# Gated delta stage re-staged: output product one stage later, first transposes last, two decay buffers; layer norms in two halves

## The reference

```python
mixed = silu(causal_conv4(hidden_states @ w_qkv)); z = hidden_states @ w_z
q = l2norm(q) * DK ** -0.5;  k = l2norm(k)          # over 128, per token and head
def step(Sm, inp):
    q_, k_, v_, g_, b_ = inp
    Sm = Sm * jnp.exp(g_)[..., None, None]
    kv = jnp.einsum('bhk,bhkv->bhv', k_, Sm)
    delta = (v_ - kv) * b_[..., None]
    Sm = Sm + jnp.einsum('bhk,bhv->bhkv', k_, delta)
    o = jnp.einsum('bhk,bhkv->bhv', q_, Sm)
    return (Sm, o)
og = o * silu(z);  on = og * rsqrt(mean(og * og) + EPS) * norm_w
return on.reshape(B, S, VAL_DIM) @ w_out
```

## Time and profile before

| | |
|---|---|
| median of three runs | 5708.66 us |
| profiled execution, its own time | 5727.5 us, span 5725.7 us |
| mean granted TensorE clock | 0.916 of full speed |
| PE busy | 4930.2 us, 86% of the span |
| DVE, ACT, POOL busy | 58%, 45%, 23% |
| the 64 stages | from about 200 to 3050 us |
| the eight layer norms | some 18 us each |

### The profile page before, as it was taken

The page is one execution under the profiler, slowest core; times in us unless marked ns, Lnnn a source line. Parts: engine busy times, 40 slices in busy tenths (PEclk is TensorE's granted clock), DMA queues, the critical chain, the costliest instruction groups (busy, mean ns, idle before and its releaser), DMA issues. The chain is left out here.

```text
span 5725.7 us, 125133 instructions
## 1 busy us (share of the span) xinstructions
PE 4930.2 (86%) x50094; PEld 3447.6 (60%) x50094; DVE 3347.2 (58%) x6298; ACT 2561.0 (45%) x6894; POOL 1319.4 (23%) x1478
## 2 busy tenths in 40 slices
...
GB/s 83 16 20 21 19 20 19 20 20 19 20 19 20 20 21 18 19 20 20 22 17 49 1 1 69 1 1 0 0 21 14 15 1 13 23 1 1 1 23 15
DMA packets 50618, 103.88 MB, mean 18 GB/s; under 512 B 12832, under 2 KB 20192, under 8 KB 48768
## 3 DMA queue, kind: packets, MB, share of 16 engines
...
## 5 line engine op out<-in xcount | busy, mean ns | idle before, releaser
L1034 DVE SCALAR_TENSOR_TENSOR dh_kq<-bank,dh_conv_kq,dh_kq 128x511 f32<-128x511 f32 (+2 forms) x408 | 305.3, 748 | 180.7 <-ACT dh_kq L850 169.6
L1034 DVE SCALAR_TENSOR_TENSOR dh_v<-bank,dh_conv_v,dh_v 128x511 f32<-128x511 f32 (+2 forms) x384 | 285.8, 748 | 169.9 <-ACT dh_v L850 159.9
L596 PE MATMUL bank<-hT,dh_w_kq 128*128 128x512 f32 x544 | 277.6, 635 | 49.3 <-DVE dh_kq L1034 42.3
L1247 POOL TENSOR_TENSOR dh_pto<-dh_qkm,dh_et 128x512 f32<-128x512 f32 x128 | 160.4, 1274 | 647.5 <-PE bank L572 647.5
L596 PE MATMUL bank<-hT,dh_w_vz 128*128 128x512 f32 x512 | 264.1, 641 | 51.0 <-DVE dh_v L1034 51.0
L1101 DVE TENSOR_TENSOR dh_turned<-dh_turned,bank 128x256 f32<-128x256 f32 x384 | 153.8, 414 | 246.8 <-ACT dh_turned L895 245.1
L1776 PE MATMUL bank<-moe_h_split,moe_w 128*128 128x512 bf16 x1200 | 277.2, 381 | 14.3 <-PEq L89 14.3
L766 PE MATMUL bank<-dh_wo_gated,dh_ww 128*128 128x256 f32 x1040 | 272.6, 421 | 0.8 <-ACT dh_ww L941 0.8
L259 POOL TENSOR_TENSOR ln_rstd<-ln_var_eps,nhalf 128x16 f32<-128x16 f32 x8 | 23.2, 2903 | 1018.3 <-DVE ln_var_eps L249 1018.3
L608 PE MATMUL bank<-dh_w_vz,hT 128*128 128x256 f32 x1024 | 245.5, 383 | 0.0
L766 PEld LDWEIGHTS bank<-dh_wo_gated,dh_ww 128*128 128x128 f32 x1040 | 214.2, 211 | 38.3 <-issue 1.1
...
## 6 DMA issues: line engine op xcount, KB each, us to landing
...
moe_w<-in_L_w13T SPq DMA_DIRECT2D x1, 3200.0 KB, 16.1
...
```

What stands on the lines that cost most here:

```text
L596: last = pe.matmul(pj_bank(n), w[:, kk, :], k.hT[:, kk, n % NB, :], start=(kk == 0), stop=(kk == KD - 1))
L1034: dve.scalar_tensor_tensor(y, pj_bank(n)[:, 0:S - i], taps(n)[:, TAPS - 1 - i:TAPS - i], y, ALU.mult, ALU.add).then_inc(s["v_cs" if i < TA ...
L1247: pool.tensor_tensor(pto[j][:, :, :], qkm[:, :, :], et[j][:, :, :], ALU.mult).then_inc(h["p_pt"], 1)
```

## The change

It computes the same. In the delta stages:
- `w_out(t - 1)` and `collect(t - 1)` stand in stage t, behind its first `next_power` and `next_turned`; they stood at the end of stage t - 1. An epilogue does the last.
- `flip(t)` and `turned_start` stand at the end of stage t, ahead of `y_turn`; they stood at the start of stage t + 1. `flip` writes the other bank (`turn_bank`).
- `decay` works in place on one of two buffers `et`, and stands in mid-stage; it stood ahead of `kk_mask` and `start_power`, read `inj` and wrote one buffer.
- `norms` is gone. `squares` does four ACTIVATEs with an accumulated sum, into `ss`, in place of one; no DVE work is left in it.
- The corner's matmuls alternate between two 64x64 tiles of the array, one for each head; both heads' matmuls ran on one tile, one head behind the other. For head 1 a third copy in `diagonal` is new.
- The filler stands in other places: `project(0)` and `project(1)` ahead of `v_turn`, `project_z(4)` and `(5)` in kind 3 (they were in kind 2), `turn_kq` 4 to 7 at the end of kind 3 (they were spread over it).

In `layernorm`, statistics, variance and the power on POOL are done for eight tiles, then for the other eight.

```diff
     def flip(pe, t):
         for j in HEADS:
-            after(pe, hs[j]["v_u"], t)
-            after(pe, hs[j]["a_u12"], t)
+            pe.wait_ge(hs[j]["v_u"], order(t) + 1)
+            after(pe, hs[j]["a_xs"], t + 1)
...
     def corner(pe, t):
...
-            for b in range(NB):
-                last = pe.matmul(pow_bank(j)[LO, b, :], off[j][HI, b, :], ttb[j][HI, b, HI], start=True, stop=True)
+        for b in range(NB):
+            for j in HEADS:
+                moved = c_even[j][LO, b, :] if j else ttb[j][HI, b, HI]
+                last = pe.matmul(pow_bank(j)[halves[j], b, :], off[j][halves[1 - j], b, :], moved, start=True, stop=True)
         last.then_inc(s["t_u12"], 1)
...
     def v_turn(pe, t, j):
-        after(pe, s["v_acc"], t)
+        pe.wait_ge(s["v_acc"], t + 1)
...
     def squares(act, q, n):
         if n < NC - 1:
-            act.activation(kt[:, par, n, :, :], b4(PJ_B), ACT.Copy)
-        if q >= 0:
-            act.wait_ge(s["t_wo"], NC * q + (2 if n < NC else 3))
-        after(act, s["v_ss"], N - 1)
-        act.activation(ww[n % 2][:, :, :], b4(PJ_B), ACT.Square).then_inc(s["a_sq"], 1)
+            act.activation(kt[:, par, n, :, :], b4(PJ_B), ACT.Copy).then_inc(s["a_kt"], 1)
+            act.wait_ge(s["a_kt"], (NC - 1) * max(q, 0) + n + 1)
+        for b in range(NB):
+            last = act.activation(b4(PJ_B)[:, b, :], b4(PJ_B)[:, b, :], ACT.Square,
+                                  accum_out=ss[:, par, n // NC, n % NC, b:b + 1])
+        last.then_inc(s["a_sq"], 1)
...
     def diagonal(act, t, j):
         for half in halves:
             last = act.activation(ttb[j][half, :, half], pow_bank(j)[half, :, :], ACT.Copy)
+        if j:
+            last = act.activation(c_even[j][LO, :, :], pow_bank(j)[HI, :, :], ACT.Copy)
...
     def decay(dve, t, j):
-        after(dve, h["p_nt"], t + 1)
-        after(dve, h["p_pt"], t + 1)
-        dve.tensor_tensor_scan(et[j][:, :, :].rearrange("p b n -> p (b n)"), ar[j][:, :],
-                               inj[j][:, :, :].rearrange("p b n -> p (b n)"), 0.0, ALU.mult, ALU.add)\
-            .then_inc(h["v_et"], 1)
+        dve.tensor_tensor_scan(e, ar[j][:, :], e, 0.0, ALU.mult, ALU.add).then_inc(h["v_et"], 1)
...
     def vector_stage(dve, t):
-        if a == 0: convolve(dve, q, 0)
-        if a == 1: scaled_out(dve, q)
-        if a == 2: convolve(dve, q, 12)
         for j in HEADS: grow(dve, t, 0, j)
+        if a == 1: scaled_out(dve, q)
+        collect(dve, t - 1)
+        if a == 0:
+            convolve(dve, q, 0)
+            convolve(dve, q, 1)
+        if a == 2: convolve(dve, q, 12)
+        for j in HEADS: grow(dve, t, 1, j)
+        if a:
+            for j in HEADS: decay(dve, t, j)
         if old:
             for j in HEADS: rhs(dve, t, j)
```

More of the change, by code:

```diff
@@ L495, in delta_pipeline @@
     per = lambda name: [sb(f"{name}{j}", [P, NB, P]) for j in HEADS]
-    inj, et, vs, ttb = per("inj"), per("et"), per("vs"), per("ttb")
+    et = [[sb(f"et{i}{j}", [P, NB, P]) for j in HEADS] for i in range(2)]
+    vs, ttb = per("vs"), per("ttb")
     pto, x0, zz, ww, yy, St = per("pto"), per("x0"), per("zz"), per("ww"), per("yy"), per("S")
@@ L680, in inverse @@
         for b in range(NB):
-            for j in HEADS:
-                at = halves[j]
-                last = pe.matmul(turn_bank(j)[LO, b, 0, :], c_odd[j][at, b, :], turn[j][at, TS[5], b, :], start=True, stop=True)
+            for at, j in zip(halves, HEADS):
+                last = pe.matmul(turn_bank(j)[at, b, 0, :], c_odd[j][at, b, :], turn[j][at, TS[5], b, :], start=True, stop=True)
         last.then_inc(s["t_t11"], 1)
@@ L761, in w_out @@
         c = rec_chunk(t)
-        for i in HEADS: pe.wait_ge(hs[i]["a_yt"], t + 1)
+        for i in HEADS: after(pe, hs[i]["a_yt"], t + 1)
         if c == 0:
@@ L810, in tensor_stage @@
             project(pe, q, 10)
+        if a == 2: turn_kq(pe, q, 2)
+        if a == 3: turn_kq(pe, q, 4)
+        for j in HEADS: pu(pe, t, j)
+        inverse(pe, t)
+        if a == 0: project(pe, q, 6)
+        if a == 1: project_z(pe, q, 3)
         if a == 2:
-            turn_kq(pe, q, 1)
             project(pe, q, 15)
-        if a == 3: turn_kq(pe, q, 6)
-        next_power(pe, t, 4)
-        next_turned(pe, t, 4)
+            turn_kq(pe, q, 3)
+        if a == 3:
+            turn_kq(pe, q, 5)
+            turn_kq(pe, q, 6)
         if a:
             for j in HEADS: ku(pe, t, j)
-        if a == 0:
-            project(pe, q, 5)
-            project(pe, q, 6)
-        if a == 1: project_z(pe, q, 3)
-        if a == 2:
-            turn_kq(pe, q, 2)
-            turn_kq(pe, q, 3)
-        if a == 3: turn_kq(pe, q, 7)
-        inverse(pe, t)
-        kk_prod(pe, t)
-        qk_prod(pe, t)
-        if a == 1: project(pe, q, 11)
-        if a == 2: project_z(pe, q, 4)
-        corner_left(pe, t)
+        kk_prod(pe, t)
+        corner_left(pe, t)
+        qk_prod(pe, t)
+        if a == 0: project(pe, q, 7)
+        if a == 1: project(pe, q, 11)
+        if a == 3: turn_kq(pe, q, 7)
+        corner(pe, t)
+        flip(pe, t)
         for j in HEADS: y_turn(pe, t, j)
-        if a == 0: project(pe, q, 7)
-        if a == 2: project_z(pe, q, 5)
-        corner(pe, t)
-        for j in HEADS: w_out(pe, t, j)
     def tap(act, q, n):
@@ L965, in scalar_stage @@
             silu(act, q, 12)
-            squares(act, q, 0)
-        if a == 3: squares(act, q, 4)
-        for j in HEADS: keep_power(act, t, 2, j)
-        for j in HEADS: keep_turned(act, t, 2, j)
+            tap(act, q, 13)
+        if a == 3: silu_z(act, q, 6)
+        for j in HEADS: z_copy(act, t, j)
+        for j in HEADS: keep_power(act, t, 3, j)
+        for j in HEADS: keep_turned(act, t, 3, j)
         if a == 0:
             silu(act, q, 1)
-            tap(act, q, 3)
+            tap(act, q, 4)
         if a == 1:
```

265 lines of the change are left out of this document (131 added, 134 removed).

## The result

The changed kernel takes 5795 us (median of four runs, 5784 to 5800), the kernel before 5709 us beside it. The ratio is 1.0138, with an interval from 1.0119 to 1.0157: 1.4% slower. 5787 us (5650 to 5880) was forecast. The profiled execution took 5791.0 us, with a span of 5789.3.

The account below looks back on a forecast made before the run. TensorE's work was taken as the floor, its waits as what can be had. 16 x (4.6 waits-less-work + 1.5 clock) = +98 us, layer norms -21, sum +77: 5787 us, 1.4% slower, range 5650 to 5880.

Parts of the forecast that it names:

- The two long waits: TensorE waits 5.5 us at turn_kq(6) for squares(5) in kind 3, 3.4 us at project(2) for convolve(0) in kind 0.
- the second wait: Kind 0, project(2): convolve(0) done at 14.6 us into the stage, TensorE there at 11.3, wait 3.4 us.
- The other waits: Shorter TensorE waits at grow, z_prod, project(14) and the corner, such as 1.7, 1.1, 1.8 and 2.3 us in kind 2.
- The corner's term: corner_left and corner on two tiles take 0.54 instead of 1.07 us, 4.3 us less TensorE work a round.
- the walk: Each engine's new order followed with row durations and 0.15 us between engines, noting where TensorE waits; round 175.9 us, was 171.3.
- the 25.1 us: TensorE's new waits summed over a round of four stages, where 16.1 us were before.
- The first rival: Waits stay at 16.1 us a round, so only work and norms count: 5619 us; 17 in 100.
- Contention: Rival: start_power, beside GpSimd's normed, takes 2.50 instead of 1.74 us every stage, 49 us more, 5836 us; 15 in 100.
- Clock: Low clock behind the two long waits costs 2.8 us each a round; 6.9 us instead of 5.4, 1.5 more.
- Layer norms: In halves, VectorE's 3.01 us wait for the power shrinks by 2.65 us, eight times, 21 us less.
- At the start of the first stage and the end of the last no change: Ends of the stage loop: no time change, since w_out only moves into the epilogue.

Follow-up runs that it names:

- moving three calls: Changed kernel with squares(5) ahead of mean_sq in kind 3, and in kind 0 v_turn between project(0) and project(1), convolve(1) behind grow(1): 5668 us, ratio 0.9914 to before.
- the run with its order mended: Changed kernel with, in kind 0, v_turn between project(0) and project(1) and convolve(1) behind grow(1): 5746 us, ratio 1.0065 to the kernel before.
- its mended order: Changed kernel with squares(5) ahead of both mean_sq on ScalarE in kind 3: 5697 us, ratio 0.9975 to the kernel before.
- the pair with `rhs` first: Changed kernel with calls reordered in kinds 0, 2, 3 and rhs ahead of kind 2's decay scans; corner on two tiles 0.9857, on one tile 0.9835.
- the run with one tile: Changed kernel with the corner back on one tile, without the fifth copy in diagonal: 5773 us, ratio 1.0093 to the kernel before.
- kernels with mended orders: Changed kernel with calls reordered in kinds 0, 2, 3: 5626 us (0.9840); the same plus rhs ahead of kind 2's scans, corner on one tile: 5617 us (0.9835).
- the fastest: Changed kernel with calls reordered in kinds 0, 2, 3, rhs ahead of kind 2's decay scans, corner back on one tile: 5617 us, ratio 0.9835 to before.

## Why the prediction came true, and where it did not

**The two long waits** were right in place and size: 5.7 us forecast as 5.5, 3.25 as 3.4. For `squares` I had taken 1.4 us, and it takes 1.27 with the step to TensorE; `mean_sq` takes 2.65 us and not 2.44. The sum for the second wait does not come out of its own terms (9.8 + 2.17 + 0.74 + 2.31 is 15.0 and not 14.6, and 14.6 - 11.3 is 3.3), so its size is partly luck. That the two waits make the loss is shown: moving three calls takes 2.2% off, more than the change had cost, and puts the kernel below the one before.

**The other waits.** `convolve(12)` ahead of `grow(1)` and `inverse` behind `grow(4)` came as walked (1.6 and 1.5 us for 1.7 and 1.6), and the corner's in kind 0 is 2.17 us (2.1 forecast). `z_prod` in kind 2 waits at most 0.6 us, where 1.1 was forecast. Kind 1 took 40.0 us (39.7 forecast) and kind 2 45.0 (45.1). Kind 0 at full clock is 46.0 + 1.7 = 47.7 (the run with its order mended, plus the wait that this took away), as forecast; kind 3 by the same reckoning is 40.3 and the 3.7 us of waits that its mended order took away ((91.0 - 26.3)/16 = 4.0 from the two lists of waits, less (76.4 - 70.6)/16 = 0.4 for the third wait for `left_copy`), 44.0, where 43.4 was forecast. Over 63 stages the forecast comes to 68 us less work, 142 us more waits and 24 us more low clock, 96 with its rounding. The table has 82 less, 131 more and 24 more: 72 us. All three went the way forecast; the first two are each more than 10 us off towards faster.

**The corner's term** (1.07 us x 4 = 4.3 us a round, 69 us, "on the engine that bounds") is the step that failed. What it takes off TensorE's work is near the forecast: 47 us over the stages in the pair with `rhs` first, 62 in the changed kernel. From one row's start to the next `corner_left` goes from 1.07 to 0.61 us, where 0.54 was forecast, and `corner` with `flip` behind it from 1.84 to 1.37; in kind 1 the stage gets 0.7 us shorter. What failed is the premise that less work of TensorE is less time: its waits grew by 63 and 60 us. In kinds 0 and 2 TensorE waits for ScalarE right at the corner, in kind 3 just ahead of it at `turn_kq(6)`, and two tiles give ScalarE more to do. In the new order the corner costs 26 us where it was to save 69; in the old one it saves 22.

The total was right all the same, in part because the walk had five copies in ScalarE's chain and the corner's waits (2.1 and 2.3 us) in the 25.1 us: it charged a gain in one column and a part of its loss in the other. Only a part: my own reckoning ahead of the run with one tile still had the two tiles ahead by 25 us. A reader of the sum alone would have kept the corner and would have been wrong.

**The first rival** (5619 us if the waits stay as they were) is ruled out for this change. The kernels with mended orders reach its number (5626 and 5617 us), but not by its sum of 69 us of work and 21 of norms. Against the kernel before, the 63 stages of the fastest have 15 us less work, 27 less waits and 58 less low clock, and it has no corner on two tiles. How much of this the new structure is needed for stays open: the orders of the kernel before were not mended in the same way, nor was moving `w_out` and `flip`, or the two decay buffers, run alone.

**Contention** went the other way. `start_power` was to be 2.50 us for four instead of 1.74. By groups of VectorE's instructions, before:

```profile
L1091 DVE TENSOR_TENSOR dh_c<-dh_kkm,dh_et 64x256 f32<-64x256 f32 x256 | 150.1, 586 | 9.5
```

Now, where it always takes the low value:

```profile
L1091 DVE TENSOR_TENSOR dh_c<-dh_kkm,dh_et 64x256 f32<-64x256 f32 x252 | 105.8, 420 | 9.3
```

420 ns on the mean over 252, or 1.7 us for four; before, single ones took up to 1.17 us. The step that failed here is its place: it was to fall beside `normed`, and it does so in no stage. It stands beside GpSimd's operations on 8 columns in kinds 0, 1 and 2 (the power among them) and beside none in kind 3. The Trainium skill, "GPSIMD Engine Reference", section 1, has VectorE's instructions with two SBUF inputs contend with GpSimd. The trace of before agrees for GpSimd's multiplications over 512 and 256 columns, and neither trace shows anything of it beside a power of 8 or 16 columns (1.74 us for four in the earlier trace rows was beside one of 16). What `start_power` would take beside `normed` is not shown.

**Clock.** +24 us forecast; the time at 1.2 GHz in the 63 stages went from 172 to 225 us, which by the prediction's reckoning (half of it lost) is 27 us. The stretches behind the two long waits are mostly shorter than forecast in kind 0 (3.4 us in 13 of 16), and others stand at the corner. Both orders mended take the low clock out of kinds 0 and 3 in most rounds. Of the 16 waits of 2.17 us at the corner of kind 0, 9 come with a stretch at 1.2 GHz in the changed kernel, the round shown among them (from 1511.7 to 1515.1 us), and 4 in the run with kind 0 mended. What decides stays open.

**Layer norms.** 21 us forecast; 20 measured (13 to 27), and 2.88 us each by the rows, which is 23.

**"At the start of the first stage and the end of the last no change"** was wrong at both ends. The changed kernel does one `w_out` more: its first stage has one for the stage ahead of it. So the one of the last stage comes on top, in the epilogue, where nothing covers it and the clock is low:

```profile
3114.87 5.40 PE L774 MATMUL bank<-dh_wo_gated,dh_ww 128*128 128x256 f32 x16 [4.01 <-PEq L89]
3121.64 1.09 PE L584 MATMUL bank<-ident,dh_v 128*128 128x128 f32 x8 [1.38 <-DVE x_res L1164]
```

With the 5.40 us, the 1.38 us that `v_turn` then waits for `collect`, and 4.01 us of idle time ahead where it was 2.83, the epilogue is some 8 us longer. The first stage begins 10.5 us earlier (190.7 us instead of 201.2), 2.9 of it the first layer norm; the rest was not followed up. The stages up to the last grew by 72 us (2802.3 to 2874.7), where 63/64 of the 98 us are 96. So part of the agreement to 8 us is luck: the stages were put some 24 us too long. Between the two profiled executions the difference is 63.5 us (5791.0 - 5727.5), less than the 77 of the sum; between the medians it is 79 to 87, since the profiled execution of before, on which the sum stands, was 19 us slower than its median.
